# Fourth QKV piece one head earlier and the value tile in heads 11 and 12, in the first attention block of an AdaLN, attention and feed-forward kernel

## What is computed

```python
# _L0_cond_ref: x (16, 256, 512), 16 heads of 32
scale, shift = split(emb @ W_emb + b_emb, 2)
xn  = rms_norm(x, g_norm) * (1 + scale) + shift
q, k, v = heads(xn @ W_qkv)
q, k = rms_norm(q, g_q), rms_norm(k, g_k)          # over each head's 32 features
attn = softmax(q @ k.T * 32 ** -0.5)
o   = attn @ v
y   = o + o @ W_out
# _L0_ffn_ref
h   = gelu(bitlinear(y, w_fc))                     # ternary weights, layer norm and quantised input
out = x + bitlinear(h, w_proj)
```

## Time and profile before

| | |
|---|---|
| time, median of 3 runs | 1092.07 us (1091.48 to 1092.49) |
| the profiled execution | 1091.28 us |
| its span in the trace | 1089.4 us |
| PE busy | 1053.6 us, 97% of the span |
| DVE, ACT, POOL busy | 910.4, 802.1, 556.3 us |
| iteration 0, head loop, on PE | about 55.7 to 96.7 us |
| mean granted clock of TensorE | 0.987 of full |

### The profile page before, as it was taken

The page is one execution under the profiler, slowest core; times in us unless marked ns, Lnnn a source line. Parts: engine busy times, 40 slices in busy tenths (PEclk is TensorE's granted clock), DMA queues, the critical chain, the costliest instruction groups (busy, mean ns, idle before and its releaser), DMA issues. The chain is left out here.

```text
span 1089.4 us, 24404 instructions
## 1 busy us (share of the span) xinstructions
PE 1053.6 (97%) x9457; PEld 666.6 (61%) x9457; DVE 910.4 (84%) x1627; ACT 802.1 (74%) x1371; POOL 556.3 (51%) x370
## 2 busy tenths in 40 slices
PE   8687999999999999999999999999999999999898
PEld 2244766656566665656666665666656566665666
DVE  4888788888898888889898898989889898868667
ACT  4886877858687685868768586876958687584854
POOL 1942562908356291835629184472918447191613
PEclk9889999999999999999999999999999999999999
DMA  9913113132311313231131312113132220212100
GB/s 350 328 49 74 49 21 81 42 79 64 77 53 31 82 45 79 64 64 61 33 84 45 79 64 59 65 30 89 45 79 65 54 70 23 57 40 59 59 21 20
DMA packets 79698, 77.13 MB, mean 71 GB/s; under 512 B 8656, under 2 KB 60256, under 8 KB 79072
## 3 DMA queue, kind: packets, MB, share of 16 engines
q1 hardware_dynamic: 79552, 75.58, 25.2%
q10 hardware_dynamic: 32, 0.01, 0.0%
HBM read 41.85 MB, written 8.40 MB: 46 GB/s over the span
## 5 line engine op out<-in xcount | busy, mean ns | idle before, releaser
L996 PE MATMUL F<-yT_hi,fc_t 128*128 128x256 f16 (+1 forms) x1040 | 228.5, 272 | 1.1 <-DVE yT_lo L1407 1.1
L997 PE MATMUL F<-yT_lo,fc_t 128*128 128x256 f16 (+1 forms) x1040 | 228.1, 272 | 0.0
L719 POOL TENSOR_TENSOR rqk<-ssq,half 128x16 f32<-128x16 f32 x64 | 197.8, 3097 | 37.3 <-DVE ssq L1587 37.3
L839 PE MATMUL F<-proj_t,hs 128*128 128x512 f16 (+1 forms) x512 | 192.4, 377 | 0.0
L841 PE MATMUL F<-proj_t,hs 128*128 128x512 f16 (+1 forms) x512 | 191.8, 376 | 0.0
L1548 DVE SCALAR_TENSOR_TENSOR hs<-hg,g_inv,hs 128x512 f16<-128x512 f32 x128 | 145.1, 1142 | 31.2 <-ACT hs L1209 31.0
L680 POOL TENSOR_TENSOR acc<-acc,hg 128x512 f32<-128x512 f32 x96 | 147.2, 1533 | 14.5 <-ACT hg L1204 1.5
L687 POOL TENSOR_TENSOR acc<-acc,hq 128x512 f32<-128x512 f32 x90 | 114.2, 1268 | 13.9 <-ACT hq L1278 5.3
L1204 ACT ACTIVATE hg<-F,g_fc 128x512 f32<-128x512 f32 x128 | 87.3, 682 | 44.8 <-PE F L997 44.8
L670 POOL TENSOR_TENSOR rs<-var,half 128x1 f32<-128x1 f32 x32 | 17.6, 550 | 189.4 <-DVE var L1396 189.4
L996 PEld LDWEIGHTS F<-yT_hi,fc_t 128*128 128x128 f16 x1040 | 102.1, 98 | 20.0 <-issue 6.5
(11 more groups left out here) (259 smaller groups left out, 2747.3 us busy)
## 6 DMA issues: line engine op xcount, KB each, us to landing
stk<-qkT SPq DMA_DIRECT2D x128, 128.0 KB, 2.5
xtok<-in_x SPq DMA_DIRECT2D x17, 512.0 KB, 3.9
xT_sb<-in_xT SPq DMA_DIRECT2D x16, 512.0 KB, 3.5
stk<-qkT SPq DMA_DIRECT2D x128, 64.0 KB, 2.2
xres<-in_x SPq DMA_DIRECT2D x15, 512.0 KB, 3.7
out<-xres SPq DMA_DIRECT2D x15, 512.0 KB, 2.8
stk<-in_w_emb SPq DMA_DIRECT2D x4, 512.0 KB, 5.8
fc_t<-in_w_qkv SPq DMA_DIRECT2D x2, 1024.0 KB, 11.5
```

The source lines that it names most:

```text
L719: pool.tensor_tensor(rqk[:, n % 2, :], ssq[:, n % 2, :], half[:, :], ALU.pow).then_inc(rqk_r, 1)
L839: pe.matmul(dst, hs[:, 0, k // 2, col:col + P], proj_t[:, k, cols], start=(k == 0), stop=False)
L996: pe.matmul(dst, w, yT_hi[:, k, cols], start=(k == 0), stop=False)
L997: mm = pe.matmul(dst, w, yT_lo[:, k, cols], start=False, stop=(k == KT - 1))
```

## The change

Only tables of iteration 0 change. Piece 3 (QKV[3]) moves from steps 9 and 10 to steps 8 and 9, its squares from 11 to 10, its norm from 13 to 12, its turn from 15 to 14. Value tile 0 moves from steps 12, 14 and 15 to steps 11 and 12. The turn of head group 2 moves from 14 to 15. The first step of value tile 1 stays in step 15. What each engine does in total is the same.

```diff
 SECOND_FILLER = {2: QKV[0][0:2], 3: QKV[0][2:4], 4: QKV[1][0:2], 5: QKV[1][2:4], 6: QKV[2][0:2], 7: QKV[2][2:4],
-                 9: QKV[3][0:2], 10: QKV[3][2:4], 12: V[0][0:2], 14: V[0][2:3], 15: V[0][3:4] + V[1][0:1]}
-SECOND_SQUARE_AT, SECOND_NORM_AT = {3: 0, 5: 1, 8: 2, 11: 3}, {5: 0, 7: 1, 10: 2, 13: 3}
+                 8: QKV[3][0:2], 9: QKV[3][2:4], 11: V[0][0:2], 12: V[0][2:4], 15: V[1][0:1]}
+SECOND_SQUARE_AT, SECOND_NORM_AT = {3: 0, 5: 1, 8: 2, 10: 3}, {5: 0, 7: 1, 10: 2, 12: 3}
 SECOND_TURN_AT = {6: ("heads", 0), 7: ("piece", 0), 9: ("piece", 1), 10: ("heads", 1), 12: ("piece", 2),
-                  14: ("heads", 2), 15: ("piece", 3)}
+                  14: ("piece", 3), 15: ("heads", 2)}
```

## The result

| | before | after |
|---|---|---|
| median of 6 runs | 1091.18 us (1090.02 to 1092.49) | 1100.69 us (1099.92 to 1101.59) |
| ratio of the two, with 95% interval | | 1.0084 [1.0073, 1.0094] |
| profiled execution, its span | 1091.28, 1089.4 us | 1101.05, 1099.2 us |
| PE, DVE, ACT busy | 1053.6, 910.4, 802.1 us | 1057.4, 909.3, 802.9 us |
| mean granted clock | 0.987 | 0.983 |

The change makes the kernel 9.5 us slower by the medians. The six runs of the kernel before include the three of the table ahead of the prediction. DVE and ACT do what they did; PE is busy 3.8 us longer for the same 9457 matmuls, the first sign that part of the loss is clock.

A forecast was written before the change was run, and what follows sets the result against it. PE, busy 97% of the span, was taken as the bound, with ACT and DVE pacing loop steps 8 to 12. Order 4.8 plus clock 3.3 made 8.1 us more, 1100.2 us for the median, range 1096.4 to 1102.4.

The forecast's parts named there:

- The sum is the shift of the last turn: End of iteration 0's loop: the whole kernel's end moves as much as the turn at 96.66.
- The wait in step 8: PE reaches piece 3 before the norm of piece 1 and stands 2.84 us instead of 0.87 + 0.20.
- the walk: Stepping the new order through the loop with start-to-start distances from the old trace, at full clock; last turn at 101.42.
- The wait in step 11: PE stands at value tile 0 for the norm of piece 2, 4.33 us instead of 0.54.
- The sum at full clock, 4.76: Loop of iteration 0: turn of head group 3 at 101.42 instead of 96.66, 4.76 us later.
- The clock, 3.3 with bounds 0 and 5.1: Clock falls from the two new waits: 2.0 us for the longer, 1.3 for the shorter.
- The dip behind the loop: Existing clock fall at 106.1, when moved: costed at nothing, 0.7 us either way.
- The DMAs: Copies into stk start 1.8 us earlier than the rest moves; gain nothing.
- A clock that stays up: Rival: column sums and scores around the waits keep the clock at 1.00; 1096.8 us, chance 0.12.
- The first wait alone: Rival: only the step 8 stall counts, the norm of piece 2 coming in time; 1094.1 to 1095.8 us, chance 0.05.
- The waits filled by value work: Rival: value work fills PE's waits in steps 9 to 15; 1089.3 to 1090.2 us, chance 0.03.
- Where a fall lands: Clock falls land differently between runs, so time scatters more than the 1 us of the three runs before.

The follow-up runs named there:

- e1: Kernel before with only piece 3 moved, to steps 8 and 9; 1095.37 us, ratio 1.0039.
- e2: Kernel before with only value tile 0 moved, to steps 11 and 12; 1095.73 us, ratio 1.0038.
- e3: Changed kernel, but value tile 0 waits for the norm of piece 0 alone instead of three norms; 1097.38 us, ratio 1.0053.
- e4: Changed kernel with 12 and 18 matmuls of ones in free bank QA ahead of the waits in steps 8 and 11; 1096.31 us, ratio 1.0043.
- e7: Kernel before with value tile 0 in steps 11 and 12, waiting for the norm of piece 0 alone; 1091.68 us, ratio 0.9995.
- e5: Changed kernel with squares and norm of piece 3 back in steps 11 and 13; 1099.94 us, ratio 1.0080.
- e10: Kernel before plus e7's edits, e8's fills and 6 matmuls of ones ahead of piece 0 in step 2; 1090.01 us, ratio 0.9983.
- e6: Changed kernel with 18 matmuls of ones ahead of the wait in step 11 alone; 1097.39 us, ratio 1.0056.
- e8: Kernel before with 4, 3 and 8 matmuls of ones in three waits behind iteration 1's output projection; 1090.27 us, ratio 0.9985.

## Why the prediction was right, step by step

- *The sum is the shift of the last turn.* Right. The first feed-forward matmul comes 12.66 us behind that turn before and 12.59 after.
- *The wait in step 8.* Right: ended by the norm that ends where it ended; e1 shows it alone. The trace says 2.67 where the walk says 2.84, since I counted from when the next matmul could start and the trace from the end of the last one: the same 0.17 in the forecast and here.
- *The wait in step 11.* Right, also that it would be there without the first (e2), and that it is a cost of its own (e3). Forecast were 4.33 us; counted the same way it is 4.16, and 3.99 as the trace counts.
- *The sum at full clock, 4.76.* Right as measured by e4: 26.77 - 22.01. In the prediction's other account of it, by PE's waits, the term 0.21 has no row and no reason; the walk doesn't need it.
- *The clock, 3.3 with bounds 0 and 5.1.* Mis-sized a little: 3.91 in the profile. The first fall cost 1.4 to 1.6, against 1.3. The second cost 2.35 as what is left, against 2.0: it came 1.8 us before the end of the wait, so that some 5 of its 6.8 us lay under matmuls. In e2, the same step alone cost 2.7 to 2.8. The prediction took its sizes from the fall of the earlier trace rows, which it puts after the wait of 2.63 us; by the earlier trace rows the clock fell at 58.3, 1.4 us before that wait ended.
- *The dip behind the loop, charged at nothing, 0.7 either way.* Here it cost 0.6 to 0.7: from the first feed-forward matmul (118.23) the clock stayed low until 123.14, 4.9 us instead of 3.6, and half of the difference is 0.65.
- *The DMAs.* Right: the copies start 1.84 us earlier than the rest moves (forecast 1.8), and nothing is gained.
- The size, 8.1, was 1.4 short of the 9.5 between the medians. In the two profiles the time from scores(8) to the end differs by 9.49 us as well: 0.6 of what is missing is the loop's clock, 0.65 the dip, and some 0.2 isn't placed. The predicted time was only 0.5 off, and that is luck: the median of six runs of the kernel before is 0.9 below that of the three that I started from, which hides most of the 1.4.
- *The rivals.* A clock that stays up is the state of e4, which had to be made. The first wait alone is e1: +3.8. The waits filled by value work is e7: even where its wait is removed, it gives 0.3, not 1.9 to 2.8. My price for that rival was too high: I added up PE's waits in steps that PE doesn't pace.
- *Where a fall lands.* Behind the same wait in step 8 the clock fell 3.8 us behind scores(8) in the changed kernel and 4.3 in e1; in e5 it fell 2.2 behind, while PE still waited. The Trainium skill, "TensorE: Matmul & The Clock Gate" (Part 1: The HAM clock gate), says that the gate's count runs freely, isn't reset by the kernel, and so places the change of level differently from run to run; it says so of the rise at a kernel's start, and the prediction carried it over to a fall. These traces agree with that as far as they show it. But in no profile was one of the two falls missing, and the runs of the changed kernel (1099.92 to 1101.59) don't scatter more than the six of before (1090.02 to 1092.49), so the wider scatter that the prediction derived wasn't seen.

## What to carry to other kernels

Before an item is moved forward in an in-order queue, look up when its operand is ready: where it isn't, the engine stands and so does everything queued behind it, and here that was the work for the engines that set the pace. A walk with start-to-start distances from the trace, which first has to land on the old rows, priced this to 0.1 us in its steps. Then add the clock: a wait of 2 to 4 us on TensorE cost 0.5 to 1.2 times itself again in matmuls at 0.50, and one that can't be avoided can be filled with matmuls into a free bank.

## What the runs showed of the hardware

- In steps 8 and 11 of the loop each wait of 2.3 to 4.0 us on PE brought a stretch at 0.50, 3.4 us or 6.8 us long, in all kernels in which it wasn't filled. The stretch began inside the wait (the second of the changed kernel, e2, the first and second of e5) or up to 1.3 us behind its end (e1). A wait of 1.47 us in e3, shortly behind one of 0.86, brought one too. Single waits of up to 0.9 us amid dense work left the clock at 1.00, and so did waits of 2.19 and 1.65 us in e10 with matmuls of ones between them. The price didn't go by the wait's length (the shortest of the four, 2.32 us in e2, was the dearest) but with the time that PE was busy under the stretch: 1.4 us for 3.42 busy (e1), 1.56 for 3.42 (e6), 2.35 for 5.07 (second of the changed kernel), 2.7 to 2.8 for 5.85 (e2), each a little less than half. In e3 it was less: some 2.2 us beyond the walk's 3.0, for 6.82 busy under its two stretches.
- The work ahead of the change differs by up to 1.8 us between profiled executions of kernels that are the same there: scores(8) starts at 74.25 (e4), 74.65 (before), 74.96 (after) and 76.07 (e8). It is wise to count from a point inside the program.
